# Moving K's rotation and a bias addition to other places in GpSimd's queue of a pre-norm attention layer

## The reference, cut to what matters

```python
x = x + attn(layernorm(x))        # 16 heads of 16 channels, rope on q and k
x = x + ffn(layernorm(x))         # token shift, sigmoid gate, squared relu

def attn(x):
    q, k, v = rope(x @ Wq.T), rope(x @ Wk.T), x @ Wv.T      # split into heads
    att = softmax(q @ k.T / sqrt(16))
    return concat_heads(att @ v) @ Wu.T + bu

def rope(x):                      # pairs (xe, xo) of channels
    return xe * cos - xo * sin, xe * sin + xo * cos

def ffn(x):
    x_prev = x shifted by one token, zero at the start
    xr, xk = mu_r * x + (1 - mu_r) * x_prev, mu_k * x + (1 - mu_k) * x_prev
    return sigmoid(xr @ W_r.T) * (square(relu(xk @ W_k.T)) @ W_v.T)
```

## Time and profile before

| | us | share of the span |
|---|---|---|
| median of 3 runs | 2382.94 | |
| the profiled execution | 2388.87 | |
| its span | 2387.1 | |
| PE busy | 2172.2 | 91% |
| DVE busy | 2052.5 | 86% |
| ACT busy | 1647.6 | 69% |
| POOL busy | 1404.7 | 59% |

### The profile page before, as it was taken

The page is one execution under the profiler, slowest core; times in us unless marked ns, Lnnn a source line. Parts: engine busy times, 40 slices in busy tenths (PEclk is TensorE's granted clock), DMA queues, the critical chain, the costliest instruction groups (busy, mean ns, idle before and its releaser), DMA issues.

```text
span 2387.1 us, 48217 instructions
## 1 busy us (share of the span) xinstructions
PE 2172.2 (91%) x13084; PEld 1137.4 (48%) x13084; DVE 2052.5 (86%) x3982; ACT 1647.6 (69%) x3137; POOL 1404.7 (59%) x1184
## 2 busy tenths in 40 slices
PE   5999999999999999999999999999999999999995
PEld 4444444444454444444455454444444454444433
DVE  5889988989899898988988899898989988998862
ACT  2567777767777776767767777677777767777662
POOL 5346766555766565765655765565775556676334
PEclk7799999999999999999999999999999999999977
DMA  6544355554345553344553345553354554444400
GB/s 152 111 97 99 91 100 113 123 115 99 83 103 107 124 119 94 95 102 97 123 117 98 83 98 112 124 117 98 99 106 88 123 126 102 99 94 86 107 28 22
DMA packets 133571, 243.18 MB, mean 102 GB/s; under 512 B 24848, under 2 KB 79760, under 8 KB 120976
## 3 DMA queue, kind: packets, MB, share of 16 engines
q1 hardware_dynamic: 133264, 239.56, 44.7%
HBM read 136.71 MB, written 83.89 MB: 92 GB/s over the span
## 4 chain that ended last, share of the span: by engine, by line
POOL 28%; PE 24%; issue 20%; DVE 13%; SPq 6%; ACT 4%; DMA 3%; DVEq 1%; POOLq 0%; ACTq 0%
PE d_ps L963 11%; PE st_ps L901 7%; POOL f_lo L476 6%; DVE mx L702 5%; PE pv_ps L933 3%; POOL rope_t L426 3%; SPq L325 3%; POOL parts L446 3%; POOL yn L492 2%; SPq L336 2%; POOL xrT L455 2%; DMA q_st<-mparts 2%; PE s_ps L919 2%; DVE sums L726 2%; POOL rope_t L429 2%
## 5 line engine op out<-in xcount | busy, mean ns | idle before, releaser
L661 ACT ACTIVATE probs<-st_ps 128x512 f32<-128x512 f32 x2048 | 1153.4, 595 | 561.7 <-PE st_ps L901 557.7
L702 DVE TENSOR_REDUCE mx<-s_ps 128x1 f32<-128x512 f32 x2048 | 1330.2, 678 | 241.7 <-PE s_ps L919 240.1
L901 PE MATMUL st_ps<-q_st,k_st 50*128 50x512 f32 x2048 | 812.7, 462 | 82.5 <-ACT probs L661 36.2
L919 PE MATMUL s_ps<-k_st,q_st 48*128 48x512 f32 x2048 | 828.7, 472 | 16.8 <-DMA k_st<-parts_scratch 7.7
L901 PEld LDWEIGHTS st_ps<-q_st,k_st 50*128 50x128 f32 x2048 | 330.4, 188 | 704.5 <-ACT probs L661 457.7
L933 PE MATMUL pv_ps<-probs,v_ext 128*32 128x512 f32 x4096 | 554.1, 613 | 0.2 <-ACT probs L661 0.2
L484 POOL TENSOR_TENSOR rs<-ve,mhalf 128x2 f32<-128x2 f32 x128 | 89.7, 701 | 504.0 <-DVE mean L768 504.0
L919 PEld LDWEIGHTS s_ps<-k_st,q_st 48*128 48x128 f32 x2048 | 336.6, 189 | 52.4 <-DVE mx L702 41.8
L476 POOL TENSOR_TENSOR f_lo<-yn,f_hi 128x512 fp32r<-128x512 f32 x128 | 174.1, 1379 | 95.5 <-ACT f_hi L629 95.5
L469 POOL TENSOR_TENSOR f_lo<-attnT,f_hi 128x512 fp32r<-128x512 f32 x64 | 86.8, 1357 | 180.7 <-ACT f_hi L617 180.6
L933 PEld LDWEIGHTS pv_ps<-probs,v_ext 128*32 128x32 f32 x4096 | 81.7, 109 | 178.6 <-issue 175.0
(11 more groups left out here) (116 smaller groups left out, 3990.4 us busy)
## 6 DMA issues: line engine op xcount, KB each, us to landing
parts_scratch<-parts SPq DMA_DIRECT2D x64, 1024.0 KB, 5.4
q_st<-parts_scratch SPq DMA_DIRECT2D x128, 256.0 KB, 5.6
k_st<-parts_scratch SPq DMA_DIRECT2D x128, 256.0 KB, 6.8
xn<-in_L_attn_x_dram SPq DMA_DIRECT2D x32, 512.0 KB, 8.9
q_st<-parts_scratch SPq DMA_DIRECT2D x128, 128.0 KB, 6.9
k_st<-parts_scratch SPq DMA_DIRECT2D x128, 128.0 KB, 7.3
attnT<-attn SPq DMA_DIRECT2D x512, 32.0 KB, 2.0
y<-in_L_attn_x_dram SPq DMA_DIRECT2D x32, 512.0 KB, 5.8
```

The lines of the kernel that those rows point to most:

```text
L661: nc.scalar.activation(probs[:, u % SLOTS, j, :], st_ps[:, n % 2, :], ACT.Exp, scale=float(D) ** -0.5).then_inc(exp_done, 1)
L702: nc.vector.tensor_reduce(mx[:, col:col + 1], s_ps[:, ring_bank(n), :], AX.X, ALU.max).then_inc(max_done, 1)
L901: nc.tensor.matmul(st_ps[:, n % 2, :], k_st[par][row:row + SROWS + MROWS, slot, c * P:(c + 1) * P], q_st[par][row:row + SROWS + MROWS, slo ...
L919: nc.tensor.matmul(s_ps[:, ring_bank(n), :], q_st[at][row:row + SROWS, slot, qc * P:(qc + 1) * P], k_st[at][row:row + SROWS, slot, :], sta ...
```

## The change

On POOL, K's rotation and low parts (`rope_mults(1, ·)`, `rope_sums(1)`, `low_parts(1)`) leave the step in which K is projected and stand at the start of the next one, between the two halves of `finish` and around `low_a`. ACT's two `high` of K go with them, from (15, 1) and (15, 3) to (2, 2) and (2, 3) of the next step, the second ahead of the `v_evac(1)` that stands there. SP's store of K's parts moves from the head of the step to the place behind `move_max(b, 1)`. `add_bu` moves from the head of the step after to the end of the sequence's own step, ahead of the last `scales`. `low_r(1)` and one of the `scales` stand a little earlier, ahead of `square(0)`. No instruction is added or taken away.

```diff
@@ -363,9 +363,9 @@
                         sp.dma_start(scratch[half, t].rearrange("(k r i) (h c) -> (i h) (k r) c", k=2, r=2, h=H),
                                      parts[:, t, :, :, :].bitcast(F32).rearrange("p k r c -> p (k r) c")).then_inc(parts_out, 16)
 
-                store_parts(b.plus(1), 1 - par, 1)
                 move_attn(b.plus(-1), 3)
                 move_max(b, 1)
+                store_parts(b.plus(1), 1 - par, 1)
                 store_out()
                 load_stacks(0)
                 load_x()
@@ -393,24 +393,22 @@
             pool.wait_ge(const_ok, 1)
 
             def step(b, par):
-                def finish():
+                def finish(n):
                     s = b.plus(-2)
                     if s.active():
-                        for n in range(2):
-                            pool.wait_ge(gated, s.count(2, n + 1))
-                            t = gate[:, 2 * n:2 * n + 2, :]
-                            nc.gpsimd.tensor_tensor(t, t, y[par][:, 2 * n:2 * n + 2, :], ALU.add).then_inc(out_done, 1)
+                        pool.wait_ge(gated, s.count(2, n + 1))
+                        t = gate[:, 2 * n:2 * n + 2, :]
+                        nc.gpsimd.tensor_tensor(t, t, y[par][:, 2 * n:2 * n + 2, :], ALU.add).then_inc(out_done, 1)
 
                 def add_bu():
-                    s = b.plus(-1)
+                    s = b
                     if s.active():
                         pool.wait_ge(xres_in, s.count(16, 16))
-                        nc.gpsimd.tensor_tensor(y[1 - par][:, :, :], y[1 - par][:, :, :],
+                        nc.gpsimd.tensor_tensor(y[par][:, :, :], y[par][:, :, :],
                                                 bu_sb[:, :].rearrange("p (a c) -> p a c", a=1)
                                                 .to_broadcast([P, TC, C]), ALU.add).then_inc(bu_added, 1)
 
-                def rope_mults(t, r):
-                    s = b.plus(2)
+                def rope_mults(s, t, r):
                     if s.active() and not first(s):
                         k = 6 * t + 2 * r
                         pool.wait_ge(qk_done, s.count(4, 2 * t + r + 1))
@@ -429,8 +427,7 @@
                             nc.gpsimd.tensor_tensor(rope_t[:, 1, :], rope_t[:, 1, :], sin_sb[:, :],
                                                     ALU.mult).then_inc(rope_step, 1)
 
-                def rope_sums(t):
-                    s = b.plus(2)
+                def rope_sums(s, t):
                     if s.active() and not first(s):
                         pool.wait_ge(rope_step, s.count(12, 6 * t + 3))
                         nc.gpsimd.tensor_tensor(rot[:, t, 1, :], rot[:, t, 1, :], rope_t[:, 0, :],
@@ -439,8 +436,7 @@
                         nc.gpsimd.tensor_tensor(rot[:, t, 0, :], rot[:, t, 0, :], rope_t[:, 1, :],
                                                 ALU.subtract).then_inc(rope_step, 1)
 
-                def low_parts(t):
-                    s = b.plus(2)
+                def low_parts(s, t):
                     if s.active() and not first(s):
                         pool.wait_ge(hi_done, s.count(4, 2 * t + 2))
                         nc.gpsimd.tensor_tensor(parts[:, t, 1, :, :], rot[:, t, :, :], parts[:, t, 0, :, :],
@@ -491,33 +487,34 @@
                         pool.wait_ge(relu_done, s.count(2, o + 1))
                         nc.gpsimd.tensor_tensor(mixT[:, o, :], mixT[:, o, :], mixT[:, o, :], ALU.mult).then_inc(ksq_done, 1)
 
-                finish()
-                add_bu()
+                rope_mults(b.plus(1), 1, 0)
+                finish(0)
+                rope_mults(b.plus(1), 1, 1)
+                rope_sums(b.plus(1), 1)
                 low_a(0)
+                low_parts(b.plus(1), 1)
                 low_a(1)
+                finish(1)
                 for n in range(2):
                     scales(b.plus(-1), n, ln2_stat, ln2_scale, ve2, mean2, rs2, nm2)
 
-                rope_mults(0, 0)
-                rope_mults(0, 1)
-                rope_sums(0)
+                rope_mults(b.plus(2), 0, 0)
+                rope_mults(b.plus(2), 0, 1)
+                rope_sums(b.plus(2), 0)
                 difference(0)
                 difference(1)
                 low_f(0, 0)
                 low_f(0, 1)
-                rope_mults(1, 0)
                 low_r(0)
-                rope_mults(1, 1)
+                scales(b.plus(3), 0, ln1_stat, ln1_scale, ve1, mean1, rs1, nm1)
+                low_r(1)
                 square(0)
-                low_r(1)
-                scales(b.plus(3), 0, ln1_stat, ln1_scale, ve1, mean1, rs1, nm1)
-                low_parts(0)
+                low_parts(b.plus(2), 0)
                 square(1)
                 low_f(1, 0)
                 low_f(1, 1)
+                add_bu()
                 scales(b.plus(3), 1, ln1_stat, ln1_scale, ve1, mean1, rs1, nm1)
-                rope_sums(1)
-                low_parts(1)
 
             step(Seq(FIRST), FIRST % 2)
             for n in range(2):
@@ -587,8 +584,7 @@
                         nc.scalar.activation(rope_t[:, r, :], d_ps[:, BANK["QK"[t], r], :],
                                              ACT.Copy).then_inc(qk_done, 1)
 
-                def high(t, r):
-                    s = b.plus(2)
+                def high(s, t, r):
                     if s.active():
                         act.wait_ge(rope_step, s.count(12, 6 * t + 6 - r))
                         nc.scalar.activation(parts[:, t, 0, r, :], rot[:, t, r, :], ACT.Copy).then_inc(hi_done, 1)
@@ -645,11 +641,15 @@
                           (6, 0): [(norm2, 0)], (6, 3): [(qk_evac, 0, 0)],
                           (7, 2): [(norm2, 1)], (7, 3): [(qk_evac, 0, 1)], (8, 2): [(yT_evac, 0)],
                           (8, 3): [(yT_evac, 1)], (9, 3): [(qk_evac, 1, 0)], (10, 0): [(high_f, 0, 0)],
-                          (10, 1): [(high_f, 0, 1)], (11, 1): [(high, 0, 1)], (11, 2): [(high, 0, 0)], (10, 3): [(qk_evac, 1, 1)],
+                          (10, 1): [(high_f, 0, 1)], (11, 1): [(high, b.plus(2), 0, 1)], (11, 2): [(high, b.plus(2), 0, 0)], (10, 3): [(qk_evac, 1, 1)],
                           (11, 0): [(high_r, 0)], (11, 3): [(relu, 0)], (12, 0): [(high_r, 1)],
                           (12, 3): [(relu, 1)], (13, 1): [(high_f, 1, 0)], (13, 3): [(tanh, 0)],
-                          (14, 0): [(high_f, 1, 1)], (14, 3): [(tanh, 1)],
-                          (15, 1): [(high, 1, 1)], (15, 3): [(high, 1, 0)]}
+                          (14, 0): [(high_f, 1, 1)], (14, 3): [(tanh, 1)]}
+                if first(b.plus(2)):
+                    extras[15, 1], extras[15, 3] = [(high, b.plus(2), 1, 1)], [(high, b.plus(2), 1, 0)]
+                elif not first(b.plus(1)):
+                    extras[2, 2] = [(high, b.plus(1), 1, 1)]
+                    extras[2, 3].insert(0, (high, b.plus(1), 1, 0))
                 for u in range(UNITS):
                     for j in range(GH):
                         if b.active():
```

## The result

The changed kernel takes 2415.01 us in the median of 4 runs (2401.01 to 2418.16), the kernel before 2387.15 beside it: ratio 1.0105, with an interval of 1.0057 to 1.0153. It is slower by 1%, where 2341 us and a gain were predicted. The profiled execution took 2415.71 us, its span 2413.9.

What follows compares the result with a forecast made beforehand. PE, busy 91% of the span, was taken to set the pace, its wait for r_lo the main loss. Gains of 40.9 + 30 x (0.15 + 0 + 0 - 0.1) = 42.4 us took 2382.9 to 2341 us, range 2324 to 2358.

Steps and rivals of the forecast that it cites:

- K's multiplications leave the stretch before low_r(1): Unit 13: PE's wait for r_lo goes, 5.54 to 4.06 us; 40.9 us gained, bounds 36 and 44.
- Sums and `high` out of unit 15: Unit 15: ACT's wait for POOL's first sum goes; PE gains 0.15 us a step, between 0 and 0.45.
- `high` and the rotation in units 0 to 4, add_bu in unit 15: ACT's idle time covers `high` (0 to 0.5 lost); DVE's add_bu effects nearly cancel (0.4 gained to 0.9 lost); both 0.
- Rival 1: Unit 15: add_bu's lock on DVE reaches PE, 0.9 us a step, 27 us, giving 2368; chance 0.12.
- The end of the run: Ahead of step 0 and after step 31: nothing on the path moves, so no gain or loss.
- The store and what SP has behind it: SP's queue to unit 8: stacks 4.1 us later, row maxima slightly late; 0.1 us a step lost, bounds 0 and 1.3.
- the end of the queue: Before unit 8: DMA engines full to 958.0, the middle of 956.6 and 959.3, instead of 955; maxima about 958.4.
- 0.48 of cover: Unit 8: PE already idles 0.48 us for ACT, which covers a late start up to 959.2.
- Rival 2: Unit 8: row maxima late by the upper bound, 1.2 us more a step, 36 us, giving 2377; chance 0.10.
- Rival 3: Unit 8: store lands after 8.2 us, PE starts 4.2 us past its cover, 81 us slower, 2464; chance 0.06.

Runs made afterwards that it cites:

- after, again: The changed kernel, unaltered, in a second set of runs: 2408.3 us, ratio 1.0117 to the kernel before.
- b_bu: The kernel before with add_bu alone moved to its new place at the end of the sequence's own step: 2391.5 us, ratio 1.0001.
- b_store: The kernel before with only SP's store of K's parts moved behind move_max(b, 1): 2455.8 us, ratio 1.0292.
- a_outlate: The changed kernel with store_out alone put behind move_max(b, 2), load_x staying ahead: 2358.3 us, ratio 0.9876.
- a_stk1late: The changed kernel with load_stacks(1) put behind move_attn(b, 0): 2382.7 us, ratio 0.9982.
- b_fill: The kernel before with nine useless products on PE ahead of unit 8's first turned score: 2401.2 us, ratio 1.0066.
- b_storefill: The kernel before with SP's store moved behind move_max(b, 1) and nine useless products on PE ahead of unit 8: 2427.9 us, ratio 1.0162.
- a_xlate: The changed kernel with load_x put behind move_max(b, 2) in SP's order: 2340.6 us, ratio 0.9786.

## Why the prediction was wrong

**K's multiplications leave the stretch before low_r(1): right.** 40.9 us forecast, 44 at most; unit 13 went from 5.58 to 4.07, 45 us in 30 steps, and stands where step 30 stood.

**Sums and `high` out of unit 15: not to be told from nothing.** Units 15 and 0 together: 9.79 before, 9.71 after and 9.99 in "after, again", so between 0.08 won and 0.20 lost; forecast 0.15 won, bounds 0 and 0.45.

**`high` and the rotation in units 0 to 4, add_bu in unit 15: near the 0 forecast.** Units 2 to 4 won 0.40 us a step, the upper bound. L731 in unit 1 took 1.10 us (forecast 1.13), L767 in unit 15 took 1.13 (forecast 1.1). b_bu and the table price the parts: add_bu's move wins 0.85 in units 2 to 4, the rest of the change takes 0.45 of it there. Rival 1's lock does reach PE in b_bu, 1.18 us in units 15 and 0, but its price, 27 us, does not come: the ratio is 1.0001, and in the changed kernel units 15 and 0 are as said above. From the changed kernel:

```profile
941.73 1.10 DVE L731 TENSOR_TENSOR sums<-sums,inv 128x256 f32<-128x256 f32 x1
...
1000.47 1.13 DVE L767 TENSOR_SCALAR ve<-mv 128x2 f32<-128x2 f32 x1
```

**The end of the run: put at nothing, but it moved.** "Ahead of step 0 and after step 31 nothing is on the path that moves", said the prediction. Behind the last score of step 31 the run takes 48.6 us in the changed kernel (in "after, again" too) and 51.3 before, so 2.7 us are won there; with step 31 itself it is 5.8.

**The store and what SP has behind it: the step that failed.** It was put at 0.1 us a step with bounds 0 and 1.3; the table has 2.91 in the changed kernel and 2.42 in b_store. The place and the mechanism were named, the size was not:

- The store was right: 4.4 us to land was taken, 4.3/4.4/4.8 is what it took in the changed kernel, and the 4.1 us of delay for all that waits for it came out as 3.84.
- Then the forecast took half of store_out's 2.7 us off again, the middle between 956.6 and 959.3. Nothing came off: x lands 3.92 us later. a_outlate prices those bytes at 0.46 us, and they are not done before the stacks: store_out is issued at 953.37 in step 12 and lands at 956.55, the first stack load is issued at 955.43.
- The maxima were put 0.4 us behind the end of the queue, 958.4, which is 35.0 us into the step. They land at 37.04 in the mean. That load_stacks(1) would close up and share the DMA engines with them was overlooked; a_stk1late prices it at 0.5 to 0.6 us. The plain sum, the landing in the kernel before plus the delay, 32.77 + 4.1 = 36.9, would have come within 0.2 us; the forecast worked from the DMA share of a stretch and never looked up when the maxima land.
- PE's arrival was taken as 958.74, 35.4 us into step 12, and 0.48 of cover added. The mean is 34.86, and in the changed kernel 34.45 (units 0 to 6 and 3.91 for unit 7): the units ahead had become shorter, and this was not carried over.
- The lower clock after the stand was in no term of the sum and in no rival: about half of the 2.91 us. The cover taken, 0.48, was in turn too small, as b_fill shows; the two errors partly cancel.

Rival 2 named the right place at less than half the price. Rival 3, slower, had the right place and the wrong cause: it needed a store of 8.2 us, and put the turning point at a store of some 5.6; it turned with one of 4.4. With what the runs showed, the sum closes: 45 us from unit 13 and 12 from units 2 to 4, less 30 x 2.91 = 87, is a loss of 30, of which step 31 and the end give 6 back.

Left open: how the DMA engines share themselves among the maxima and the loads around them in detail. b_storefill kept more of its loss (42 us) than the 24 expected: in steps 4 to 27 a step is 0.81 us longer than in the kernel before, as expected (0.8), and another 10 us stand in steps 0 to 3 (286.5 us against 276.7), in the first two of which `fill` makes no products; the rest is not accounted for.

## What to carry to other kernels

When a transfer is moved in an in-order queue, write down for every small, urgent transfer behind it the time it lands and the time it is needed, both in the new schedule, and look at what is issued behind it as well as ahead: here the urgent 16 KB shared the DMA engines with megabytes on both sides. Put the urgent ones first (the same change then takes 2333 us). And price a new wait on PE with the clock that may follow it: read the granted clock behind the waits that the trace already has.

## What was not expected of the hardware

- A stand of 2.09 us on PE was followed by a granted clock of 0.50, at which the turn of Y took 1.97 us; stands of 1.24 us in a_outlate (above) and 1.01 in a_xlate left units 7 and 8 of their step 12 at 1.00. The length of the stand alone does not decide: in a_outlate one of 2.17 us (step 9) left them at 1.00, one of 1.52 (step 15) was followed by 0.87 in the mean of both units. PE of a_xlate, unit 8 of step 12:

```profile
944.00 0.52 PE L901 MATMUL st_ps<-q_st,k_st 50*128 50x512 f32 x1 [1.01 <-DMA q_st<-mparts]
```

  Nine useless products in the wait bring back 38 to 45 us of 2415. The Trainium skill (TensorE: Matmul & The Clock Gate, "HAM oscillation — how this bites in real kernels") describes a kernel in which waits for DMAs throw the clock back each time around the loop; the changed kernel's trace agrees, 0.85 over units 7 and 8 of step 12 against 1.00 before.
- PE could start on four small DMAs issued by ACT only 10.1 us after their issue, behind SP's loads, and the four issues kept ACT from computing for 2.29 us.
